# Handing 14 of the 32 tiles of a search's last count from VectorE to ScalarE, in a kernel of attention with top-k emphasis, two mixtures of experts and a state-space layer

## What is computed

```python
scores = jnp.einsum('bhqd,bhkd->bhqk', q, k) * scale * (1.0 + 0.5 * NORADRENALINE)
top_k = max(1, int(s * 0.2))                       # 102 of 512
threshold = lax.top_k(scores, top_k)[0][..., -1:]  # the 102nd largest of each row
emphasis = jnp.where(scores >= threshold, 1.0 + 0.3 * DOPAMINE, 1.0)
scores = scores * emphasis
scores_pooled = scores.mean(axis=-2)
li = conv1d(scores_pooled, conv_w) + conv_b        # over keys, per head
probs = softmax(scores * li[:, :, None, :])
ctx = probs @ v
```

## Time and profile before

| what | us |
|---|---|
| median of 3 runs | 3391.09 |
| lowest, highest | 3389.65, 3392.9 |
| the profiled execution's own time | 3393.52 |
| its span, first to last instruction | 3392.3 |
| VectorE busy | 2613.5 |
| TensorE busy | 2336.6 |
| ScalarE busy | 1557.9 |
| GpSimd busy | 1210.9 |

### The profile page before, as it was taken

The page is one execution under the profiler, slowest core; times in us unless marked ns, Lnnn a source line. Parts: engine busy times, 40 slices in busy tenths (PEclk is TensorE's granted clock), DMA queues, the critical chain, the costliest instruction groups (busy, mean ns, idle before and its releaser), DMA issues. The chain is left out here.

```text
span 3392.3 us, 34666 instructions
## 1 busy us (share of the span) xinstructions
PE 2336.6 (69%) x8947; PEld 1154.7 (34%) x8947; DVE 2613.5 (77%) x6691; ACT 1557.9 (46%) x3364; POOL 1210.9 (36%) x1118
## 2 busy tenths in 40 slices
PE   3068775876648786797758786487866876586854
PEld 1015222542215431363215531154313632164313
DVE  4874899779987799858898699977899588964282
ACT  2406722675226752467226652167524682263322
POOL 3020336314343153513454143341545143631471
PEclk8579787978869897797979887698878989697857
DMA  3011012131011311131110410113101311102212
GB/s 92 0 28 26 25 45 58 40 95 47 33 49 32 102 53 32 50 93 55 45 52 25 122 52 24 49 34 103 57 29 49 103 50 42 52 18 89 66 38 87
DMA packets 118905, 181.35 MB, mean 53 GB/s; under 512 B 15824, under 2 KB 55392, under 8 KB 115552
## 3 DMA queue, kind: packets, MB, share of 16 engines
q1 hardware_dynamic: 114528, 170.05, 17.9%
q0 software_dynamic: 4096, 8.40, 0.9%
HBM read 156.51 MB, written 21.89 MB: 53 GB/s over the span
## 5 line engine op out<-in xcount | busy, mean ns | idle before, releaser
L1324 POOL TENSOR_TENSOR gat<-sil,cbs 128x512 f32<-128x512 f32 x256 | 324.1, 1268 | 372.7 <-ACT sil L1289 272.1
L736 DVE TENSOR_SCALAR_CACHE_REDUCE wmask<-z,tc 128x512 bf16<-128x512 f16 x640 | 436.0, 741 | 23.4 <-ACT z L703 19.2
L1520 ACT ACTIVATE ps_rest<-cols,Aneg 128x512 f32<-128x512 f32 x256 | 175.8, 689 | 417.8 <-DVE hfc L1540 384.5
L904 POOL TENSOR_SCALAR wmask<-wmask 128x512 bf16<-128x512 bf16 x256 | 163.0, 637 | 482.4 <-DVE wmask L861 477.4
L1264 PE MATMUL ps_rest<-rest_hT,WF 128*128 128x512 f32 x512 | 291.2, 656 | 29.0 <-ACT sil L1289 28.8
L987 PE MATMUL ps_att<-z,Vp 128*32 128x128 f32 x2048 | 282.6, 285 | 20.2 <-DVE z L1059 20.2
L1254 PE MATMUL ps_rest<-gat,WP 128*128 128x512 f32 x512 | 280.0, 631 | 4.6 <-POOL gat L1324 4.3
L1289 ACT ACTIVATE sil<-ps_rest,w_b1T 128x512 f32<-128x512 f32 x256 | 174.1, 685 | 213.9 <-PE ps_rest L1264 209.0
L1037 DVE CUSTOM_DVE_ANT_0 z<-ps_att,wmask 128x512 f32<-128x512 f32 x256 | 175.6, 686 | 119.3 <-PE ps_att L975 111.9
L669 PE MATMUL ps_att<-qk 128*128 128x512 bf16 x512 | 221.7, 448 | 66.4 <-DVE g_rank L852 25.8
L1492 PE MATMUL ps_rest<-hg,ident 128*128 128x512 f32 x256 | 197.6, 864 | 98.9 <-DVE hg L1552 98.6
(11 more groups left out here) (358 smaller groups left out, 5280.2 us busy)
## 6 DMA issues: line engine op xcount, KB each, us to landing
cbs<-spreads SPq DMA_DIRECT2D x128, 256.0 KB, 3.4
WF<-in_w SPq DMA_DIRECT2D x64, 256.0 KB, 2.6
WP<-in_w SPq DMA_DIRECT2D x64, 256.0 KB, 2.6
WF<-in_wfc SPq DMA_DIRECT2D x64, 256.0 KB, 2.6
WG<-in_wgate SPq DMA_DIRECT2D x64, 256.0 KB, 2.9
WP<-in_wproj SPq DMA_DIRECT2D x64, 256.0 KB, 3.3
qk<-bounce SPq DMA_DIRECT2D x32, 384.0 KB, 6.0
bounce<-both_parts SPq DMA_DIRECT2D x72, 128.0 KB
```

The source lines that it names most:

```text
L736: od.up(dve.tensor_scalar(wmask[:, i, :], z_at[i], tc[:, 0, i:i + 1], None, ALU.is_ge, ALU.add, accum_out=tc[:, 1, i:i + 1]))
L1324: weighed0.up(pool.tensor_tensor(gat[m % 2], sil[m % 2], cbs[e % 2][:], ALU.mult))
L1520: decays.up(act.activation(dA[k][:], dl[:, k, :], ACT.Exp, scale=Aneg[:, k, s:s + 1]))
```

## The change

In the last round ScalarE takes 14 tiles as in the three before, and the choice reads what Sign left for them, +1 where the score is under the threshold and -1 where it is not. For those 14 tiles TensorE adds half a big number times the sign, then minus half a big number by a product with a single row of weights, then the raw scores: under the threshold the first two cancel, over it they leave -1e30. The final mask is (x >= v) >= sign. The search's threshold update ends with an OR that sets the last bit of the thresholds of the next round's sign tiles, so that none is equal to a float16 score. The order's constants change as well.

```diff
-SIGNS = (8, 14, 14, 14, 0)
+SIGNS = (8, 14, 14, 14, 14)
+BY_ACT = TILES - SIGNS[-1]
...
+    half_big = sb("half_big", [P, P], BF16); minus_half = sb("minus_half", [1, 2], BF16)
...
+        built.up(pool.memset(minus_half[:], -BIG / 2))
+        built.up(pool.memset(half_big[:], 0.0)); pool.wait_ge(*built.at(0, 19))
+        built.up(pool.affine_select(out=half_big[:], in_=half_big[:], compare_op=ALU.not_equal, fill=BIG / 2, base=0,
+                                    pattern=[[-1, P]], channel_multiplier=1))
...
-            aim.up(dve.copy_predicated(t, under, v["tn"]))
+            od.up(dve.copy_predicated(t, under, v["tn"])); od.settle()
             yield 0.24
+            odd = t[:, TILES - SIGNS[k + 1]:].bitcast(I32)
+            aim.up(dve.tensor_scalar(odd, odd, 1, None, ALU.bitwise_or))
+            yield 0.22
...
-                pe_raw(i, xbank[i % 3], False)
-                yield 0.40
-                below.up(pe.matmul(xbank[i % 3][:], minus_big[:], wmask[:, i, :], start=False, stop=True))
-                yield 0.33
+                if i < BY_ACT:
+                    pe_raw(i, xbank[i % 3], True, False)
+                    yield 0.40
+                    below.up(pe.matmul(xbank[i % 3][:], minus_big[:], wmask[:, i, :], start=False, stop=True))
+                    yield 0.33
+                else:
+                    pe.matmul(xbank[i % 3][:], half_big[:], wmask[:, i, :], start=True, stop=False)
+                    yield 0.33
+                    pe.matmul(xbank[i % 3][:], ones_bf[0:1, :], minus_half[:, 0:1].broadcast_to([1, S]), start=False, stop=False)
+                    yield 0.30
+                    below.up(pe_raw(i, xbank[i % 3], False, True))
+                    yield 0.40
...
-                n = dve_rare(dve.tensor_scalar(wmask[:, i, :], z_at[i], tc[:, 0, i:i + 1], None, ALU.is_ge), n)
+                n = dve_rare(dve.tensor_scalar(wmask[:, i, :], z_at[i], tc[:, 0, i:i + 1], None, ALU.is_ge if i < BY_ACT else ALU.is_lt), n)
...
-                                                   ALU.is_ge, ALU.add))
+                                                   ALU.is_ge, ALU.add if i - 1 < BY_ACT else ALU.is_ge))
...
-           (467.5, 1.12, (("pe", pe_choices()), ("act", act_choices()), ("dve", dve_choices()), ("pool", pool_choices()),
+           (474.0, 1.1, (("pe", pe_choices()), ("act", act_choices()), ("dve", dve_choices()), ("pool", pool_choices()),
```

More of the change, by code:

```diff
@@ L131, in emit @@
     loaded, late = sig("loaded", len(EARLY) + 1, 16), sig("late", len(LATER), 16, 30.0)
-    built, hot, cleared = sig("built", 18), sig("hot", 8), sig("cleared", 8 * FULL + 2 * E + 7)
+    built, hot, cleared = sig("built", 21), sig("hot", 8), sig("cleared", 8 * FULL + 2 * E + 7)
     siluc, modp, bop, ready = sig("siluc", 2), sig("modp", 2), sig("bop"), sig("ready", 5)
@@ L665, in dve_prepare, with pe_raw @@
             yield from dve_values(b)
-    def pe_raw(i, bank, stop):
+    def pe_raw(i, bank, start, stop):
         j, h = i % NT, i // NT
-        return pe.matmul(bank[:], qs[:, h, j * P:(j + 1) * P], ks[:, h, :], start=True, stop=stop)
+        return pe.matmul(bank[:], qs[:, h, j * P:(j + 1) * P], ks[:, h, :], start=start, stop=stop)
     def pe_refill(b):
@@ L680, in pe_refill @@
                 pe.wait_ge(*free)
-            raw.up(pe_raw(i, att.bank[i % 3], True))
+            raw.up(pe_raw(i, att.bank[i % 3], True, True))
             yield 0.40
```

## The result

Five runs of the changed kernel gave a median of **3415.99 us** (3410.33 to 3429.75), beside 3392.9 for the kernel before in the same session. The ratio is 1.0075, 95% interval 1.0055 to 1.0096: the change makes the kernel 0.75% slower. The forecast was 3352, its range ended at 3388. The profiled execution took 3413.1 us, its span is 3411.9.

The account below looks back on a forecast made before the run. VectorE's queue was taken to bound each period from search to scans. The terms -74.7 + 15.0 + 2.5 + 9.3 + 0 + 9.1 gave -38.8 us, from 3391.1 to 3352 us; the 8-in-10 range was 3325 to 3388.

Parts of the forecast that it names:

- Part 1: VectorE's queue, last count of the eight searches: fourteen counts leave it in each, -74.7 us.
- Part 2: Searches beside the experts: VectorE waits for ScalarE's signs, which stand between SiLUs, +15.0 us (ends 0 and +30).
- Part 3: VectorE turning sign sums into counts (L743) once more per search, +2.5 us.
- Part 4: The OR that makes a threshold odd, four per search, 32 in all, +9.3 us (ends +6 and +41).
- Part 5: TensorE's third product per sign tile, 112 in all, hides behind VectorE: 0 us (upper end +71).
- Part 6: The changed order around tally and experts' sum: more VectorE idle time, half given back, +9.1 us (ends 0 and +41).
- part 7: Set-up: four short GpSimd instructions before the first batch, beside loads, 0 us; ScalarE's signs left to the rivals.
- Rival B: ScalarE's queue beside the experts: signs hold up the SiLUs, 3.6 us of each period go, +25, 3377 us; chance 0.13.
- A: Rival: the rest block sets the period and takes all of the gain, -64.6, 3326 us; chance 0.20.
- C: Rival: GpSimd holds VectorE's OR, 28 of them caught at 1.257 us, +28, 3380 us; chance 0.06.
- D: Rival: TensorE becomes the choice's bound, each of the 112 third products waited for, +71, 3423 us; chance 0.09.
- E: Rival: nothing comes of it, the search's saving is waited for in the softmax's tail, 3391 us; chance 0.07.

Follow-up runs that it names:

- e14: The changed kernel with the attention's lead over the rest block at 1.12 instead of 1.1, nothing else, run as a control: 3428.18 us, 0.9999 of the kernel before.
- e18: The kernel before with signs spread among SiLUs in its third and fourth counts, one SiLU to three signs: 3428.65 us, 0.9999 of the kernel before.
- e13: The changed kernel at lead 1.12 with the last round's signs spread among the SiLUs, two signs to one SiLU: 3414.50 us, 0.9950 of the kernel before.
- e17: The changed kernel at lead 1.12 with the signs of the last three rounds spread among the SiLUs: 3400.25 us, 0.9923 of the kernel before.
- e3: The kernel before with the attention's lead at 1.1 instead of 1.12, none of the change's instructions: 3426.32 us, 1.0104 of the kernel before.

## Why the prediction was wrong

The forecast had the mechanism of the gain and its size, and missed two ways in which it is given back. Read for VectorE's queue it is 62.9 us less work (parts 1, 3 and 4) and 24.1 us more waiting (parts 2 and 6). The two profiled executions show 54.7 us less work and 74.3 us more waiting. The 8 us of work that are missing are about what the normalisations of L437 take more (10.3); the 50 us of waiting are the miss.

*Part 1* (-74.7) is right: 74.3 and 71.9 by the two runs that give the counts back. In the first search, with no rest block beside it, the sum of parts 1, 3 and 4 can be seen alone: the last addition of the first batch's attention starts at 316.1 us where it started at 323.9, 7.8 us earlier, and 7.9 were forecast. In e14, whose first choice waits for TensorE, it starts at 319.9.

*Part 2* (+15.0) was too dear. VectorE's waits for signs at the conversion, both its forms together, went from 38.5 us to 47.6, and to 40.1 in e14. *Part 3* (+2.5): 8 x (0.308 + 0.04) = 2.8. *Part 4* (+9.3): 4 to 12 by the runs. *Part 5* (0): 7 to 8 at lead 1.12; the cover fails in the first choice when the granted clock is low there.

**Part 6 and a sentence of part 7 are the steps that failed.**

"The weaver's new constants (474.0, 1.1) are in these positions and cost nothing else": they cost 18 us. With the smaller lead the second mixture begins before the softmax's last scores, and SyncE's queue, which the working never looked at, holds its weights behind eleven loads that wait for those scores.

"I let that give half of it back: 7 x 1.3 = +9.1": part 6 counted 2.6 us more idle time per period and halved it, as the rest block would gain. At equal lead the choices have 2.7 us more of it per period (53.2 to 72.1 us over seven) at 1.10 and 4.4 at 1.12, nothing is given back, and the searches have 10 to 12 us more besides. Nor is it where part 6 looked: between the first MAX8 and the experts' sum VectorE is idle for 8.2 us in all, and was for 8.5.

"ScalarE's own 112 signs are 79 us in an engine with 1834 us free; they matter by where they stand (rivals)": part 7 put them at nothing in the sum. At lead 1.12, 13.7 us come back when the last round's signs are spread among the SiLUs (e13) and 27.9 when three rounds' are (e17). At the forecast's own lead TensorE's waits for SiLUs are 57.0 us against 16.8 in e3.

With e18 and e14, both at lead 1.12 and of sessions with the same level, the account is 53.0 us less work and 48.6 more waiting, 4.4 us faster; the medians differ by nothing that can be told. The spreading of three rounds returns 28 us; what makes the rest of the waiting stays open.

*Rival B* named a mechanism that decides, the signs that hold up the SiLUs, and took a step of 7.8 us between two SiLUs; it is 7.96 here and 8.44 in e14. It was priced at 3.6 us of each period because it let TensorE catch up behind the hold at its full pace. The rows show instead products that start 1.7 to 1.9 us apart for three products, where 0.86 is usual: in e14 that alone adds (1.87 + 1.70 + 1.71) - 3 x 0.86 = 2.7 us. With 0.13 it had too little of the chances, and no rival held the lead's cost. *A* is out, since the rest block sped nothing up. *C* is out: the OR's mean is 0.204 us, once or a few times near 1.1. *D* is out for the kernel as built, whose MAX8's waits are 10.5 us; at lead 1.12 they are 26.5 in e14, 3.4 of it at sign tiles, nearly all in the first choice. *E* is half true: VectorE's share in the softmax's tail fell, as it said, but the periods grew longer; in that tail VectorE waits for TensorE's scores, and the late weights come after it.

## What to carry to other kernels

Work that is moved to an engine with half its time free still has to stand somewhere in that engine's queue. A run of it ahead of short instructions on which another engine's chain hangs can cost the run's whole length, and more if the engine that waits comes back slower, as TensorE did here; let the moved work alternate with them, and price the change by the gap between two such instructions, not by the engine's free time. When a change brings new scheduling constants, run the old kernel with them and the new one without them, and read every in-order queue that they reorder, the one that issues transfers too: a load that waits holds up all the loads behind it.

## What the runs showed of the hardware

*TensorE after a pause.* Products of 1.02 us took 2.07 and 2.08 us right after idle times of 3.95 and 4.68 us. Stretches of e14 ahead of its pause and behind it (columns as in the earlier trace rows):

```profile
1628.00:1635.00 7.00, 7.00 (x18) 3.13 (x17) 5.93 (x16) 3.56 (x9) 4.64 (x4) 1.00 0.26 75
1641.00:1646.00 5.00, 4.89 (x6) 2.14 (x7) 5.00 (x15) 4.50 (x12) 2.92 (x3) 0.50 0.01 5
```

The granted clock is 1.00 while the engine is busy throughout and 0.50, that is 1.2 of 2.4 GHz, in the work that follows the pause. So this wait of 4.68 us cost 7.4 with what followed.

*The one-row product.* Rows of the changed kernel (duration ns min/median/max):

```profile
L814 PE MATMUL ps_att<-minus_half,ones_bf x112: 384/602/604, 186.3 to 2954.8; 1*128 1x512 bf16 x112
```

```profile
L812 PE MATMUL ps_att<-wmask,half_big x112: 379/607/634, 186.0 to 2954.2; 128*128 128x512 bf16 x112
```

A product over one row takes as long as its neighbour over 128. The Trainium skill (TensorE: Matmul & The Clock Gate, Why this matters for your kernels) says this of 32 rows; by these rows it holds down to one.

*Transfers behind transfers.* The gate weights issued at 1885.10 us, right behind eleven stack loads, landed 11.7 us later, against a median of 3.0 from issue to landing. In the last three sessions the kernel before took 37 us longer than in the first two, on one chip in both ways (3391.5 and 3428.5), and in e18, which has its constants and nearly its order, TensorE waits 16.2 us for the gate weights where the trace of before has 2.1; why these weights came later there stays open.
